# A projected tensor stored with 8 channels innermost between a projection and a depthwise convolution

## The chip, the cores and the metric

The kernel runs on one core of one Trainium2 chip. The metric is the device time of one execution in microseconds (us). Engines are named as the profile names them: PE is the matrix engine (PEld its weight loads), DVE the vector engine, ACT the scalar engine, POOL the GpSimd engine, SP the sync engine, which here only issues transfers. SBUF is the on-chip memory, PSUM the accumulator that PE writes.

## The reference

```python
# x: 16 images, 192 channels, 56 x 56
def _L0_conv_ref(x, ...):          # quantized window attention, windows of 7 x 7, 12 heads
    ...
    out = quant_linear(out, Wout, bout)                       # the projection
    return out.reshape(B, r1, r2, WS, WS, C).transpose(0, 5, 1, 3, 2, 4).reshape(B, C, H, W)

def _L1_conv_ref(x, ...):
    y = jax.lax.conv_general_dilated(x, dw_w, window_strides=(1, 1), padding=[(3, 3), (3, 3)],
                                     feature_group_count=C)   # 7 x 7, each channel by itself
    y = y + dw_b[None, :, None, None]
    ...                             # layer norm over channels, 192 -> 768, gelu, norm, 768 -> 192
    return residual + y
```

## The kernel before, in words

The kernel is a sequence of phases: `phase_input`, `phase_qkv_range`, `phase_qkv`, `phase_range`, `phase_attention`, `phase_project`, `phase_conv`, `phase_mlp`. Each writes its result to DRAM and the next reads it from there. Inside a phase every engine has its own instruction stream, written out by hand, and the streams meet at semaphores. The change touches `phase_project`, `phase_conv` and the DRAM tensor `yd` between them.

**phase_project** works on one image after the other, the buffers of two images in turn (index `k`). The attention result of an image comes as two units (`o_in`, 588 KB a transfer, four transfers an image), POOL rounds it to 16 bits (`o_int`, L1036), PE transposes it in bands of 7 image rows (L1082, 8 transposes of 128 columns a band, 8 bands an image, for the image that comes next), and DVE places each band into `oT` (L1202, two instructions a band). From `oT` two products are formed:

- `y` (L1098): the projection with a pair of image rows (two rows of 64 positions) on the 128 partitions and the 192 output channels in the free dimension. One step x of the loop makes two row pairs (q = 2x, 2x + 1), each out of two matmuls of 192 columns (96 + 3 and 96 input rows), in one PSUM bank; 29 row pairs make NY = 15 steps, of which the last has one pair. The moving operand is `woutT`, the stationary one `oT`. Two banks are used in turn, so PE waits at step x until DVE has done step x - 2 (semaphore `ye`).
- `r` (L1106): the same projection with channels on partitions, 448 positions at a time, 14 steps an image, two matmuls each. It is the residual and is evacuated by ACT (L1134).

The `y` product is kept as two 16-bit parts. ACT (L1125) writes the high part of both row pairs, 384 elements, in one instruction. DVE (L1215) then computes product times scale minus high part, one instruction of 192 elements a row pair, so two a step. The tile `y_out` is `[P, NCB, 2, CB, QP]`: 24 blocks of CB = 8 channels, the two parts, 8 channels, QP = 29 row pairs innermost. Neighbouring channels are therefore 29 elements, 58 bytes, apart, and ACT and DVE write (and DVE also reads) with that step. At the end of an image POOL issues the store of `y_out` to `yd` (L1047, 2784 KB) and of `r_out` to `rd` (L1049, 2352 KB).

PE's order in a step x is: the y matmuls, the r matmuls, then (x even) the transposes of one band of the next image. ACT's order is y part, r part. DVE's order is the low parts of step x, then (x even) the placing of a band.

**phase_conv** takes a block of 8 channels at a time, 24 blocks, double buffered: SP loads `c_in` from `yd` (1856 KB, all 16 images), two banded weight matrices (`toeplitz`, 1024 KB each, L1253) and the bias, after the block before the last has been evacuated. The convolution over the rows and columns of a row pair is a product with a 128 x 128 banded matrix; d = 0, 1, -1, 2 are the offsets in row pairs. Each channel takes 4 x 3 = 12 matmuls (L1282) into its own PSUM bank: three for each offset (high weight by high part, high by low, low by high), 448 columns for d = 0 and 1, 432 for d = -1 and 2. The moving operand is `c_in[:, images, part, ch, lo+d:hi+d]`, 16 runs of 28 or 27 neighbouring 16-bit elements, and every matmul has its own weight load. ACT evacuates a channel with L1296 into `c_out`, a 32-bit tile whose innermost dimension is the 8 channels, so with a step of 32 bytes. POOL stores the block (1792 KB, L1263).

**Other places that matter as comparisons.** In the attention and range phases the product L533 takes its stationary operand from `k_diag` with `[:, j::UP]`, UP = 16 elements of bf16, a step of 32 bytes over 128 columns. In `phase_qkv` DVE copies 8-bit values to bf16: L508 in order, L511 with the source read at a step of 49 bytes and written in runs of four. In `phase_mlp` L1485 and L1521 read 448 neighbouring elements as moving operand; L1688 is the same operation as L1215 (scale, subtract the high part, 16-bit result) on 448 neighbouring elements.

Of the kernel before, what the change touches and what calls it, by code (L numbers as in the profile page):

```python
# [39 lines left out]
CB = 8  # L40
# [39 lines left out]
def setup(nc, a, ctx):  # L80
# [22 lines left out]
    s.od = s.dram("od", [UNITS, 2, N, UP, 2, CK], F32)  # L103
    s.yd = s.dram("yd", [NCB, P, IMG, 2, CB, QP], F16)
    s.zd = s.dram("zd", [IMG, P, NCB, ROWP, CB], F32)
# [838 lines left out]
def phase_project(s):  # L944
# [3 lines left out]
    with ExitStack() as c:  # L948
# [4 lines left out]
        ot = [[sb(f"oT{t}_{k}", [CK + NPART * (t == 0), ROWS, PITCH], BF16) for t in range(2)] for k in range(2)]  # L953
        y = [sb(f"y_out{k}", [P, NCB, 2, CB, QP], F16) for k in range(2)]
        r = [sb(f"r_out{k}", [CK, 2, TOK], F32) for k in range(2)]
# [58 lines left out]
        def _(pool):  # L1014
# [24 lines left out]
            def image(i, first, has_next):  # L1039
                for k in range(2):  # L1040
                    m = 2 * i + k
                    if has_next(1):
                        for hf in range(2):
                            quantize(2 * m + 4 + hf, hf, False)
                    pool.wait_ge(ye, NY * (m + 1))
                    pool.wait_ge(re, 2 * NTC * (m + 1))
                    pool.dma_start(s.yd[:, :, bass.ds(m, 1)].rearrange("b p i x c q -> p (b i) (x c q)"),  # L1047
                                   y[k][:].rearrange("p b x c q -> p b (x c q)")).then_inc(sty[k], 16)
                    pool.dma_start(s.rd[bass.ds(m, 1)].rearrange("i (t p) n -> (i p) t n", t=2), r[k][:]).then_inc(strr[k], 16)  # L1049
# [10 lines left out]
        def _(pe):  # L1060
# [27 lines left out]
            def image(i, first, has_next):  # L1088
                for k in range(2):
                    m = 2 * i + k  # L1090
                    pe.wait_ge(otd, 16 * (m + 1))
                    for x in range(NY):
                        if not (first and k == 0 and x < 2):
                            pe.wait_ge(ye, NY * m + x - 1)
                        for qq in range(2 * x, min(2 * x + 2, QP)):
                            for t in range(2):
                                rows = ot[k][t][:, ROWS - 2 * qq - 2:ROWS - 2 * qq, :].rearrange("p r x -> p (r x)")
                                last = nc.tensor.matmul(py[:, (x + k * NY) % 2, qq % 2 * C:(qq % 2 + 1) * C], rows, s.woT[t][:],  # L1098
                                                        start=t == 0, stop=t == 1)
# [14 lines left out]
        def _(act):  # L1114
            act.wait_ge(ch, LCH)

            def image(i, first):
                for k in range(2):
                    m = 2 * i + k
                    for x in range(NY):  # L1120
                        act.wait_ge(ym, NY * m + x + 1)
                        if not first and x == 0:
                            act.wait_ge(sty[k], 16 * i)
                        nq = min(2, QP - 2 * x)
                        nc.scalar.activation(y[k][:, :, 0, :, 2 * x:2 * x + nq].rearrange("p b c q -> p q b c"),  # L1125
                                             py[:, (x + k * NY) % 2, 0:nq * C].rearrange("p (q b c) -> p q b c", b=NCB, c=CB),
                                             ACT.Copy, scale=ysc[:]).then_inc(yh, 1)
# [11 lines left out]
        def _(dve):  # L1139
# [67 lines left out]
            def image(i, first, has_next):  # L1207
                for k in range(2):
                    m = 2 * i + k
                    for x in range(NY):  # L1210
                        dve.wait_ge(yh, NY * m + x + 1)
                        nq = min(2, QP - 2 * x)
                        for qq in range(nq):
                            part = y[k][:, :, :, :, 2 * x + qq]
                            last = v.scalar_tensor_tensor(part[:, :, 1], py[:, (x + k * NY) % 2, qq * C:(qq + 1) * C].rearrange("p (b c) -> p b c", c=CB),  # L1215
                                                          ysc[:], part[:, :, 0], ALU.mult, ALU.subtract)
                        last.then_inc(ye, 1)
                        if has_next(k) and x % 2 == 0:
                            place(m + 1, 1 - k, x // 2, first and k == 0)
# [3 lines left out]
def phase_conv(s):  # L1223
# [5 lines left out]
    with ExitStack() as c:  # L1229
        sb = lambda n, sh, dt: c.enter_context(nc.sbuf_tensor(n, sh, dt))  # L1230
        yi = [sb(f"c_in{k}", [P, IMG, 2, CB, QP], F16) for k in range(2)]
        tp = [sb(f"toeplitz{k}", [P, 2, CB, D, P], F16) for k in range(2)]
# [9 lines left out]
        def _(sp):  # L1242
            def block(i, first):
                for k in range(2):
                    n = 2 * i + k
                    if not first:
                        sp.wait_ge(ev, CB * (n - 1))
                    sp.dma_start(yi[k][:], s.yd[bass.ds(n, 1)].rearrange("b p i x c q -> (b p) i x c q")).then_inc(ld[k], 16)
                    for x in range(2):
# [19 lines left out]
        def _(pe):  # L1269
            def block(i, first):  # L1270
                for k in range(2):
                    n = 2 * i + k
                    pe.wait_ge(ld[k], 64 * (i + 1))
                    for ch in range(CB):
                        if not (first and k == 0):
                            pe.wait_ge(ev, CB * (n - 1) + ch + 1)
                        out = ps[:, ch, 0:IMG * ROWP].rearrange("p (i r) -> p i r", i=IMG)

                        for x, d in enumerate((0, 1, -1, 2)):
                            lo, hi = max(0, -d), min(ROWP, QP - d)  # L1280
                            for part, (w, yy) in enumerate(((0, 0), (0, 1), (1, 0))):
                                last = nc.tensor.matmul(out[:, :, lo:hi], tp[k][:, w, ch, 2 - d, :], yi[k][:, :, yy, ch, lo + d:hi + d],  # L1282
                                                        start=x == 0 and part == 0, stop=x == 3 and part == 2)
                        last.then_inc(mm, 1)
# [515 lines left out]
```

## Time and profile before

| | |
|---|---|
| median of 3 runs | 6250.11 us (6248.59 to 6251.65) |
| the profiled execution, span from first to last instruction | 6255.8 us |
| PE busy | 4613.8 us (74%), 34250 instructions |
| DVE busy | 4853.0 us (78%), 8894 instructions |
| ACT busy | 3365.4 us (54%), 5458 instructions |
| POOL busy | 1553.1 us (25%), 1645 instructions |
| phase_project, by the first and last y product and low part | 3217 to 3822 us |
| wait for the last store and the first loads of the convolution | 3822 to 3859 us |
| phase_conv, its matmuls | 3859 to 4359 us |

For the profiled execution the trace gives the span alone; 6255.8 us is 5.7 us above the median of the runs. In the profile a row of the grouped view names line, engine, operation, out<-in, shapes and count, then the busy time in us and the mean of one in ns, then the idle time of the engine before them and what ended it. The granted PE clock is given as a share of full speed.

### The profile page before, as it was taken

To read this page: it belongs to the slowest core of one execution; us is meant where nothing else is said; L and a number is where in the kernel's file an instruction comes from. 1 tells how busy PE (TensorE), PEld (TensorE's weight loads), DVE (VectorE), ACT (ScalarE), POOL (GpSimd) and SP (SyncE) were. 2 spreads that over 40 slices of the span, in tenths; PEclk is the share of its full clock that TensorE was granted. 3 is DMA by queue.
4 is the path that set the end of the run, shared out by engine and by line. 5 is a ranking of instruction groups with operands and counts; after the bars stand their busy time and mean duration, and the time that the engine had idled before them with its cause. 6 is when DMAs were issued, how large, how long until landed. Compare 5 with 4: busy or idle time off the path is not lost. (4 is left out here: it accounts for less than half of the span.)

```text
span 6255.8 us, 106546 instructions
## 1 busy us (share of the span) xinstructions
PE 4613.8 (74%) x34250; PEld 2551.4 (41%) x34250; DVE 4853.0 (78%) x8894; ACT 3365.4 (54%) x5458; POOL 1553.1 (25%) x1645
## 2 busy tenths in 40 slices
PE   0879975555466666666647775998599998999989
PEld 0435543222255554554535453443233333333333
DVE  5989988999999888988968883000778778787784
ACT  1746650000177777777748885443455555555553
POOL 1013320000155555555532220000212112121120
PEclk9995555555599999999965556999799999999999
DMA  7846662333332222222235555887111212212111
GB/s 285 222 120 186 193 178 51 65 62 62 57 79 70 70 76 73 71 69 73 63 115 201 197 195 197 281 276 260 55 56 64 79 56 70 74 53 89 56 62 56
DMA packets 226353, 721.81 MB, mean 115 GB/s; under 512 B 34954, under 2 KB 132746, under 8 KB 205194
## 3 DMA queue, kind: packets, MB, share of 16 engines
q1 hardware_dynamic: 182346, 523.09, 29.3%
q0 software_dynamic: 43584, 193.63, 9.2%
q8 instruction: 197, 3.23, 0.2%
q14 instruction: 226, 1.85, 0.1%
HBM read 426.68 MB, written 289.92 MB: 115 GB/s over the span
## 5 line engine op out<-in xcount | busy, mean ns | idle before, releaser
L861 ACT ACTIVATE attn_int<-p_psum,scalars 128x588 int8<-128x588 f32 x512 | 384.2, 750 | 1174.9 <-PE p_psum L533 1174.2
L785 POOL TENSOR_TENSOR exp_lo<-exp,exp_hi 128x294 f16<-128x294 f32 x1024 | 826.9, 830 | 646.5 <-ACT exp_hi L855 644.8
L1570 ACT ACTIVATE gelu<-h_psum,b_rows,w_unscale 128x448 f32<-128x448 f32 x672 | 485.3, 722 | 669.7 <-PE h_psum L1485 548.6
L1521 PE MATMUL out_psum<-gelu_hi,w_parts 128*128 128x448 f16 x2016 | 622.3, 364 | 8.3 <-DVE w_parts L1707 4.4
L826 PE MATMUL o_psum<-a_v,exp_hi 128*128 128x68 f16 x3072 | 286.0, 202 | 444.9 <-DVE a_o L906 437.3
L533 PE MATMUL range_psum<-q_diag,k_diag 128*128 128x196 bf16 x1536 | 364.6, 373 | 331.0 <-DVE p_min L651 328.8
L1613 DVE BATCH_NORM_STATS2 ln_stats<-z_img 128x6 f32<-128x192 f32 x448 | 125.5, 337 | 555.7 <-DMA z_img<-zd 555.7
L1685 DVE TENSOR_SCALAR gelu_hi<-gelu,h_scale 128x448 f16<-128x448 f32 x672 | 323.5, 486 | 284.5 <-ACT gelu L1570 276.8
L1125 ACT ACTIVATE y_out<-y_psum,y_scale 128x384 f16<-128x384 f32 (+1 forms) x240 | 453.4, 1889 | 145.8 <-PE y_psum L1098 141.1
L1282 PE MATMUL conv_psum<-c_in,toeplitz 128*128 128x448 f16 (+1 forms) x2304 | 476.4, 369 | 62.2 <-DMA dwb<-in_L_conv_dw_b_dram 59.6
L1485 PE MATMUL h_psum<-ln_parts_T,w_hi 128*128 128x448 f16 x2016 | 502.0, 359 | 18.1 <-DVE w_in L1676 17.3
L880 DVE SCALAR_TENSOR_TENSOR logit_int<-attn_int,scalars,bias_products 128x588 f16<-128x588 int8 x512 | 442.9, 865 | 92.1 <-issue 58.8
L1215 DVE SCALAR_TENSOR_TENSOR y_out<-y_psum,y_scale,y_out 128x192 f16<-128x192 f32 x464 | 442.1, 1151 | 91.0 <-ACT y_out L1125 88.7
L1521 PE MATMUL out_psum<-gelu_lo,w_parts 128*128 128x448 f16 (+1 forms) x1344 | 499.6, 373 | 0.0
L1688 DVE SCALAR_TENSOR_TENSOR gelu_lo<-gelu,h_scale,gelu_hi 128x448 f16<-128x448 f32 x672 | 457.8, 695 | 0.0
L1485 PE MATMUL h_psum<-ln_parts_T,w_lo 128*128 128x448 f16 x1344 | 440.1, 361 | 0.0
L826 PEld LDWEIGHTS o_psum<-a_v,exp_hi 128*128 128x128 f16 x3072 | 220.8, 101 | 514.7 <-DVE a_o L906 477.6
L1296 ACT ACTIVATE c_out<-conv_psum,dwb,conv_unscale 128x448 f32<-128x448 f32 x192 | 223.4, 1163 | 315.2 <-PE conv_psum L1282 315.2
L854 ACT ACTIVATE exp<-l_psum,scalars 128x588 f32<-128x588 f32 x512 | 381.2, 744 | 21.7 <-PE l_psum L812 20.7
L855 ACT ACTIVATE exp_hi<-l_psum,scalars 128x588 f16<-128x588 f32 x512 | 391.9, 765 | 0.0
L533 PEld LDWEIGHTS range_psum<-q_diag,k_diag 128*128 128x128 bf16 x1536 | 180.9, 159 | 514.5 <-DVE p_min L651 511.1
L651 DVE TENSOR_TENSOR p_max<-range_psum,p_max 128x588 f32<-128x588 f32 x512 | 383.9, 750 | 0.0
(306 smaller groups left out, 10448.7 us busy)
## 6 DMA issues: line engine op xcount, KB each, us to landing
k_diag<-kd SPq DMA_DIRECT2D x128, 384.0 KB, 5.2
toeplitz<-gd SPq DMA_DIRECT2D x48, 1024.0 KB, 17.2
yd<-y_out POOLq DMA_DIRECT2D x16, 2784.0 KB, 20.9
c_in<-yd SPq DMA_DIRECT2D x24, 1856.0 KB, 9.1
zd<-c_out POOLq DMA_DIRECT2D x24, 1792.0 KB, 13.7
z_img<-zd SPq DMA_DIRECT2D x16, 2688.0 KB, 9.7
x_chunk<-in_x_dram SPq DMA_DIRECT2D x12, 3136.0 KB, 9.8
x_img<-in_x_dram SPq DMA_DIRECT2D x16, 2352.0 KB, 16.0
```

The source lines that it names most:

```text
L533: last = nc.tensor.matmul(out[:, g, 0:HG * N], kt[:, g].rearrange("p o n -> p (o n)")[:, j::UP], q[:, g, :, j * N:(j + 1) * N], start=True ...
L785: last = nc.gpsimd.tensor_tensor(el[r][:, :, a, 0:N], src[:, :, a], eh[r][:, :, a, 0:N], ALU.subtract)
L826: last = nc.tensor.matmul(po[:, b * PV0:(b + 1) * PV0], x[r][:, b].rearrange("p a n -> p (a n)"), rhs, start=x is eh, stop=x is el)
L855: nc.scalar.activation(eh[r][:].rearrange("p b a n -> p a b n")[:, :, :, 0:N], pl[:, bank, 0:HM].rearrange("p (a b n) -> p a b n", a=2, b= ...
L880: v.scalar_tensor_tensor(a2[r][:], a1[(l - LAG_A2) % 2][:], col(s, RAT), s.bpart[:], ALU.mult, ALU.add).then_inc(a2d, 1)
L1125: nc.scalar.activation(y[k][:, :, 0, :, 2 * x:2 * x + nq].rearrange("p b c q -> p q b c"), py[:, (x + k * NY) % 2, 0:nq * C].rearrange("p ...
L1215: last = v.scalar_tensor_tensor(part[:, :, 1], py[:, (x + k * NY) % 2, qq * C:(qq + 1) * C].rearrange("p (b c) -> p b c", c=CB), ysc[:], p ...
L1282: last = nc.tensor.matmul(out[:, :, lo:hi], tp[k][:, w, ch, 2 - d, :], yi[k][:, :, yy, ch, lo + d:hi + d], start=x == 0 and part == 0, sto ...
L1485: last = nc.tensor.matmul(ph[:, y % 3, 0:TCH], w, xx, start=x == 0, stop=x == 4)
L1521: last = nc.tensor.matmul(po[0:rows, t, 0:TCH], w, hx[:, f, cols], start=f == 0 and x == 0, stop=f == NF - 1 and x == len(steps) - 1)
L1570: nc.scalar.activation(h[y % 3][:], ph[:, y % 3, 0:TCH], ACT.Gelu, scale=k1[:], bias=b1[:, f:f + 1]).then_inc(hd, 1)
L1688: v.scalar_tensor_tensor(hl[:, f - 1, cols], h[(y - 1) % 3][:], kh[:], hh[:, f - 1, cols], ALU.mult, ALU.subtract).then_inc(hld, 1)
```

## The change

The dimension order of `yd`, `y_out` and `c_in` becomes row pairs, then channels: 8 channels are innermost (16 bytes). The y matmuls write their PSUM bank in the order block, row pair, channel, so that a block's row pairs lie next to each other. ACT's high part has runs of 16 neighbouring elements on both sides. DVE's low part becomes one instruction of 384 elements a step. The convolution's moving operand steps over row pairs, 8 elements or 16 bytes. Transfers, buffers, semaphores and their counts stay.

```diff
-    s.yd = s.dram("yd", [NCB, P, IMG, 2, CB, QP], F16)
+    s.yd = s.dram("yd", [NCB, P, IMG, 2, QP, CB], F16)
...
-        y = [sb(f"y_out{k}", [P, NCB, 2, CB, QP], F16) for k in range(2)]
+        y = [sb(f"y_out{k}", [P, NCB, 2, QP, CB], F16) for k in range(2)]
...
-                        for qq in range(2 * x, min(2 * x + 2, QP)):
+                        nq = min(2, QP - 2 * x)
+                        both = py[:, (x + k * NY) % 2, 0:nq * C].rearrange("p (b q c) -> p q b c", q=nq, c=CB)
+                        for qq in range(nq):
+                            top = ROWS - 2 * (2 * x + qq) - 2
                             for t in range(2):
-                                rows = ot[k][t][:, ROWS - 2 * qq - 2:ROWS - 2 * qq, :].rearrange("p r x -> p (r x)")
-                                last = nc.tensor.matmul(py[:, (x + k * NY) % 2, qq % 2 * C:(qq % 2 + 1) * C], rows, s.woT[t][:],
+                                rows = ot[k][t][:, top:top + 2, :].rearrange("p r x -> p (r x)")
+                                last = nc.tensor.matmul(both[:, qq], rows, s.woT[t][:].rearrange("p (b c) -> p b c", c=CB),
                                                         start=t == 0, stop=t == 1)
...
-                        nc.scalar.activation(y[k][:, :, 0, :, 2 * x:2 * x + nq].rearrange("p b c q -> p q b c"),
-                                             py[:, (x + k * NY) % 2, 0:nq * C].rearrange("p (q b c) -> p q b c", b=NCB, c=CB),
+                        nc.scalar.activation(y[k][:, :, 0, 2 * x:2 * x + nq, :].rearrange("p b q c -> p b (q c)"),
+                                             py[:, (x + k * NY) % 2, 0:nq * C].rearrange("p (b x) -> p b x", b=NCB),
                                              ACT.Copy, scale=ysc[:]).then_inc(yh, 1)
...
-                        for qq in range(nq):
-                            part = y[k][:, :, :, :, 2 * x + qq]
-                            last = v.scalar_tensor_tensor(part[:, :, 1], py[:, (x + k * NY) % 2, qq * C:(qq + 1) * C].rearrange("p (b c) -> p b c", c=CB),
-                                                          ysc[:], part[:, :, 0], ALU.mult, ALU.subtract)
-                        last.then_inc(ye, 1)
+                        hi, lo = (y[k][:, :, h, 2 * x:2 * x + nq, :].rearrange("p b q c -> p b (q c)") for h in range(2))
+                        v.scalar_tensor_tensor(lo, py[:, (x + k * NY) % 2, 0:nq * C].rearrange("p (b x) -> p b x", b=NCB),
+                                               ysc[:], hi, ALU.mult, ALU.subtract).then_inc(ye, 1)
...
-        yi = [sb(f"c_in{k}", [P, IMG, 2, CB, QP], F16) for k in range(2)]
+        yi = [sb(f"c_in{k}", [P, IMG, 2, QP, CB], F16) for k in range(2)]
...
-                                last = nc.tensor.matmul(out[:, :, lo:hi], tp[k][:, w, ch, 2 - d, :], yi[k][:, :, yy, ch, lo + d:hi + d],
+                                last = nc.tensor.matmul(out[:, :, lo:hi], tp[k][:, w, ch, 2 - d, :], yi[k][:, :, yy, lo + d:hi + d, ch],
                                                         start=x == 0 and part == 0, stop=x == 3 and part == 2)
```

The two transfers of `yd` (L1047 and L1248) follow the new order; each moves the same runs of neighbouring bytes as before.

## Rows read from the trace of the kernel before

**Rows 1.** Busy time by stretch: projection, gap, convolution, and a stretch of phase_qkv.
```profile
core 0: us, PE busy (x) PEld busy (x) DVE busy (x) ACT busy (x) POOL busy (x), PEclk, DMA share, GB/s
3217.00:3822.00 605.00, 437.16 (x2332) 291.93 (x2330) 513.04 (x704) 526.99 (x464) 122.42 (x90) 0.55 0.55 188
3822.00:3859.00 37.00, 0.51 (x2) 0.28 (x3) 0.00 (x0) 0.00 (x0) 2.10 (x2) 0.50 0.81 269
3859.00:4359.00 500.00, 475.86 (x2304) 224.80 (x2301) 0.00 (x0) 223.17 (x192) 26.55 (x23) 0.99 0.80 267
547.00:625.00 78.00, 77.88 (x324) 46.44 (x323) 76.56 (x117) 54.39 (x115) 30.64 (x36) 0.50 0.67 195
```

**Rows 2.** Waits in the projection: total us, times, longest.
```profile
PEld y_psum L1098 <- DVE y_out L1215: 256.7, 212, 3.4
...
PE y_psum L1098 <- DVE y_out L1215: 115.6, 159, 1.8
DVE y_out L1215 <- ACT y_out L1125: 88.7, 120, 3.0
```

**Rows 3.** Two steps of the projection in order of time (start us, us, instruction).
```profile
3500.49 1.94 DVE L1215 SCALAR_TENSOR_TENSOR y_out<-y_psum,y_scale,y_out 128x192 f16<-128x192 f32 x2 [0.38 <-ACT y_out L1125]
...
3502.49 0.82 PE L1098 MATMUL y_psum<-woutT,oT 99*128 99x192 bf16 x4 [0.75 <-DVE y_out L1215]
...
3503.10 0.95 PE L1106 MATMUL r_psum<-oT,woutT 99*96 99x448 bf16 x2
3503.34 1.93 ACT L1125 ACTIVATE y_out<-y_psum,y_scale 128x384 f16<-128x384 f32 x1
...
3503.85 1.06 PE L1082 MATMUL oT_psum<-ident_f,o_int 128*96 128x128 f16 x8
```

**Rows 4.** Groups by line and shape, whole trace: the projection's instructions and contiguous ones like them.
```profile
L1688 DVE SCALAR_TENSOR_TENSOR gelu_lo<-gelu,h_scale,gelu_hi 128x448 f16<-128x448 f32 x672 | 457.8, 695 | 0.0
...
L1215 DVE SCALAR_TENSOR_TENSOR y_out<-y_psum,y_scale,y_out 128x192 f16<-128x192 f32 x464 | 442.1, 1151 | 91.0 <-ACT y_out L1125 88.7
L1125 ACT ACTIVATE y_out<-y_psum,y_scale 128x384 f16<-128x384 f32 x224 | 435.9, 1946 | 145.8 <-PE y_psum L1098 141.1
...
L861 ACT ACTIVATE attn_int<-p_psum,scalars 128x588 int8<-128x588 f32 x512 | 384.2, 750 | 1174.9 <-PE p_psum L533 1174.2
...
L472 ACT ACTIVATE qk_i<-qk_psum,qk_quant_scale 128x392 int8<-128x392 f32 x384 | 196.6, 580 | 56.0 <-PE qk_psum L448 55.8
...
L1134 ACT ACTIVATE r_out<-r_psum,res_const,scale_y 96x448 f32<-96x448 f32 x224 | 195.1, 871 | 0.0
...
L1202 DVE TENSOR_SCALAR oT<-oT_psum 96x392 bf16<-96x392 f16 x256 | 131.7, 591 | 16.1 <-PE oT_psum L1082 16.1
```

**Rows 5.** Two stretches of 20.8 us inside the convolution.
```profile
3912.40:3933.20 20.80, 20.80 (x104) 10.05 (x103) 0.00 (x0) 9.84 (x9) 1.15 (x1) 1.00 0.77 243
3933.20:3954.00 20.80, 19.11 (x95) 8.99 (x93) 0.00 (x0) 8.78 (x8) 1.15 (x1) 1.00 0.91 308
```

**Rows 6.** PE alone in phase_mlp, contiguous moving operand (start us, us).
```profile
5001.44 0.54 PE L1521 MATMUL out_psum<-gelu_hi,w_parts 128*128 128x448 f16 x2
5001.82 0.35 PE L1521 MATMUL out_psum<-gelu_lo,w_parts 128*128 128x448 f16 x1
5002.01 0.54 PE L1521 MATMUL out_psum<-gelu_hi,w_parts 128*128 128x448 f16 x2
```

**Rows 7.** Groups by line and shape, whole trace: instructions with a step, and their contiguous neighbours.
```profile
L1570 ACT ACTIVATE gelu<-h_psum,b_rows,w_unscale 128x448 f32<-128x448 f32 x672 | 485.3, 722 | 669.7 <-PE h_psum L1485 548.6 <-issue 121.1
...
L1296 ACT ACTIVATE c_out<-conv_psum,dwb,conv_unscale 128x448 f32<-128x448 f32 x192 | 223.4, 1163 | 315.2 <-PE conv_psum L1282 315.2
...
L511 DVE CAST k_out<-qk_i 128x392 bf16<-128x392 int8 x128 | 129.5, 1012 | 4.0
...
L508 DVE CAST q_out<-qk_i 128x392 bf16<-128x392 int8 x128 | 45.6, 356 | 0.0
```

**Rows 8.** Weight loads in the attention phase: contiguous (L826) and with a 32-byte step (L533).
```profile
L826 PEld LDWEIGHTS o_psum<-a_v,exp_lo 128*128 128x128 f16 x2940 | 220.3, 100 | 0.0
...
L533 PEld LDWEIGHTS p_psum<-q_diag,k_diag 128*128 128x128 bf16 x1470 | 152.0, 149 | 73.6 <-issue 73.6
```

More of the change, by code:

```diff
@@ L1046, in image @@
                     pool.wait_ge(re, 2 * NTC * (m + 1))
-                    pool.dma_start(s.yd[:, :, bass.ds(m, 1)].rearrange("b p i x c q -> p (b i) (x c q)"),
-                                   y[k][:].rearrange("p b x c q -> p b (x c q)")).then_inc(sty[k], 16)
+                    pool.dma_start(s.yd[:, :, bass.ds(m, 1)].rearrange("b p i x q c -> p (b i) (x q c)"),
+                                   y[k][:].rearrange("p b x q c -> p b (x q c)")).then_inc(sty[k], 16)
                     pool.dma_start(s.rd[bass.ds(m, 1)].rearrange("i (t p) n -> (i p) t n", t=2), r[k][:]).then_inc(strr[k], 16)
@@ L1247, in block @@
                         sp.wait_ge(ev, CB * (n - 1))
-                    sp.dma_start(yi[k][:], s.yd[bass.ds(n, 1)].rearrange("b p i x c q -> (b p) i x c q")).then_inc(ld[k], 16)
+                    sp.dma_start(yi[k][:], s.yd[bass.ds(n, 1)].rearrange("b p i x q c -> (b p) i x q c")).then_inc(ld[k], 16)
                     for x in range(2):
```

## The prediction

> **What bounds the kernel now.** I cut the span into phases first, because the change touches two of them and leaves the other six as they are. The busy time by stretch [rows 1] shows the projection, 605 us: ACT busy 527 us, DVE 513 us, PE 437 us at a granted clock of 0.55 (so mostly at 1.2 GHz), the DMA engines 55% of the time. No engine is full, so the bound must be a loop between them. The waits [rows 2] name it: PE's y product waits 115.6 us for DVE's low part (its weight load 256.7 us), DVE 88.7 us for ACT's high part. Two PSUM banks are used in turn, so step x + 2 of PE needs DVE's step x. The order in time [rows 3] gives one turn: DVE's two low parts from 3500.49 for 1.94 us, PE's four matmuls from 3502.49 for 0.82 us, ACT's high part from 3503.34 for 1.93 us, then DVE again at about 3505.3: 4.8 us for two steps, 2.4 a step. 15 steps and a boundary make 605/16 = 37.8 us an image.
>
> The convolution is different. Its 500 us have PE busy 476 us at clock 0.99, with the DMA engines at 80% [rows 1]. In its full stretches 104 matmuls start in 20.8 us, in the others 95 [rows 5]: 200 ns a matmul, or 219 where loads are late. 96 matmuls at 200 ns are 19.2 us of the 500/24 = 20.8 us of a block. PE sets this phase almost alone, and the transfers follow closely.
>
> So the change makes cheaper what bounds the projection and touches, in the convolution, the one operand whose streaming bounds that phase.
>
> **The projection, removed work.** The low part: 464 instructions of 1151 ns go [rows 4], 240 of 384 elements come. The same operation on 448 neighbouring elements costs 695 ns (L1688) [rows 4]. Fewer elements, but one operand from PSUM: I take 650 ns. The high part: 1946 ns now for 384 elements with a 58-byte step. Contiguous evacuations with one scale cost 580 ns for 392 elements and 750 for 588 [rows 4]; I take 600 ns. Runs of 16 instead of one long run may add a little; the ends are 550 ns and 900.
>
> **What is next in line there.** Four sums for one image, in its engines' own durations:
> - PE: 58 y matmuls of 192 columns, 28 r matmuls of 448, 64 transposes of 128, together 31,872 columns. At the half clock, which 0.55 says it nearly always has, these are 26.6 us. (Check in [rows 3]: 8 transposes in 1.06 us, 107 ns apart plus one latency.)
> - ACT: 15 x 0.60 + 14 x 0.87 (L1134 [rows 4]) = 21.2 us.
> - DVE: 15 x 0.65 + 16 x 0.59 (L1202 [rows 4]) = 19.2 us.
> - DMA: 0.55 x 605/16 = 20.8 us of pure transfer.
>
> PE becomes the longest. The old loop shrinks to 0.65 + 0.82 + 0.60 = 2.1 us for two steps, but in the worst order it also waits behind ACT's r part (0.87) and DVE's placing (1.2): 4.1 us for two steps, 31 us an image, against 3.5 for PE's columns. PE alone with 1.8 us for the turn of images (last band transposed, placed, first product) gives 28.4 us. I take the middle, 29.7 us, 475 us in all: **130 us saved**. Ends: 31 us an image and more trouble with the transfers, 60 us saved; or the clock goes to its upper level and ACT's 21.2 us bind, 340 us, 265 saved. Against that second end speaks a stretch of phase_qkv where PE is busy 77.88 of 78 us and the clock still reads 0.50 [rows 1]: a fuller PE does not by itself bring the upper level.
>
> POOL's order (round two units, wait for the image, issue the two stores) is not moved; its roundings wait for PE's transposes and come earlier with them. SP's loads likewise. The stores keep their runs of bytes, so L1047's packets cost what they did. The y matmuls now write PSUM in runs of 8 columns with a gap of 8: the nearest row is the convolution's own, which writes 16 runs, and I cost it at nothing; if each such write took double, 58 x 192 columns would add 9.3 us an image and take the whole gain of this phase. PE has no cover for it once it is the bound.
>
> **The convolution, the changed read.** 2304 matmuls of 440 columns on average. Now one takes 200 ns: 183 ns of columns at 2.4 GHz plus 17. In phase_mlp, with one contiguous run of 448, three matmuls start in 5002.01 - 5001.44 = 0.57 us, 190 ns each against 187 of columns [rows 6]. So 16 short runs already cost some 14 ns more than one long one, about 0.9 ns at each jump. After the change each of the 440 elements is its own jump of 16 bytes. No row shows a moving operand with a step; the bounds:
> - Below: nothing. The trace has no step as short as 16 bytes, and the jumps above may have another cause.
> - By PE's jumps: 0.9 ns an element, 396 ns more a matmul, 38 us a block, 24 x 38 = 912 us, less the 1.6 us a block that PE now waits: some 870.
> - By ACT's writes with a 32-byte step: 1163 ns against 722 for 448 elements [rows 7], 0.98 ns more an element. A contiguous element costs ACT (750 - 580)/196 = 0.87 ns [rows 4], so a step costs it a little over double per element.
> - By DVE's read with a 49-byte step: 1012 against 356 ns for 392 elements [rows 7], 1.67 ns more; on PE 735 ns a matmul, some 1690 us. This is the upper end.
> - By PE's own other read: 128 weight columns at a 32-byte step take 149 ns against 100 [rows 8], 0.38 ns more a column, which nearly doubles PE's 0.42 ns.
>
> ACT's ratio (its element time slightly over doubled) and PE's weight loads (0.38 ns more a column) agree, and the last row is the nearest since it is PE reading 16-bit data from SBUF. I take a doubled column: 440 x 0.83 = 367 ns plus 8, 375 ns a matmul, 36.0 us a block. Transfers (0.80 x 20.8 = 16.7 us a block) and ACT (8 x 1.16 = 9.3 us) lie well inside. 24 x 36.0 = 864 us instead of 500: **364 us lost**.
>
> The Trainium skill has a rule on this (page "SBUF — State Buffer", section "Door 1: The DMA port swizzle", the note on cachelines): SBUF has lines of 16 bytes, full bandwidth wants at least two accesses to a line, and every move to a new line is penalised. By it the change falls exactly on one access a line, and the sum is of the sign that I give. ACT's row with a 32-byte step agrees.
>
> The gap of 37 us between the phases (store and first load) keeps its length; phase_mlp reads `zd`, which is unchanged.
>
> **The sum.** -130 + 364 = +234 us. On the profiled span: 6255.8 + 234 = 6490; the runs' median is 5.7 us lower, so 6484 us. With the bounds of this case (60 to 265 saved; 0.8 to 0.9 ns a column, 340 to 410 lost), its own range is 6325 to 6600.
>
> **Rivals.**
> - *The 16-byte step is free.* The convolution stays 500 us and only the projection moves: 6250 - 130 = 6120, or 5985 to 6190. This is faster, by one mechanism in one place: PE's fetch of the moving operand at L1282. It decides from a price of about 0.6 ns a column: the gain of 130 us over 24 x 96 x 440 = 1.01 million columns is 0.13 ns each, on top of today's 200/440 = 0.45. For it: 16 bytes is shorter than every step in rows 7 and 8, and weight loads could be slower for reasons of their own. Against it: three different engines pay for a step in this trace. The same note of the Trainium skill also says that 8 bf16 elements can be strided for free; taken at its word that is this rival, 6120 us, and no run here shows it yet.
> - *The step costs three times or more a column.* By PE's jump price 6250 - 130 + 870 = 6990, by DVE's read up to 7810. For it: the jump price is from the very same matmuls. Against it: the weight loads, where 128 such columns fit in 149 ns altogether, latency included.
> - *The projection gains nothing*, because PSUM writes in runs of 8 columns double the y matmuls, or the loop of waits stays: then +364 stands alone, 6614. For: nothing in the rows; against: the sizes of L1215 and L1125, which can only fall.
>
> **How the numbers follow.** Doubled column 0.46; free step (with mild prices below 0.6 ns) 0.35; three times or more 0.16; no gain in the projection beside a slow convolution 0.03. The likeliest case gives the time, 6484 us. To hold 8 in 10 the range must take in the free step's middle and leave out the third case: 6030 to 6600. Faster by over 0.2% (12.5 us, about what a measurement of this kernel can tell from no change): 0.35. Within: 0.01. Slower: 0.64.
>
> **What would show it.** L1282: start to start near 375 ns and a convolution phase near 864 us, its mean duration some 180 ns above 373; if it stays at 200 ns, the free step is right; near 600, the third case. The granted clock of that phase is of interest, since a read-bound PE would not need the upper level. L1215 as 240 instructions near 650 ns, L1125 near 600. In the projection the waits of L1098 on L1215 nearly gone, PE over 90% busy at 0.5 to 0.6, and 475 us. If L1098's matmuls start further apart than 160 ns, the PSUM pattern costs something. The prediction is wrong if a column of the convolution costs under 0.6 ns.

## The result: 18% slower, and the profile after

The changed kernel takes 7395.85 us, median of 4 runs (7381.1 to 7400.09), against 6250.88 us for the kernel before in its 4 runs. The ratio is 1.1826 with a 95% interval of 1.1809 to 1.1843. The forecast was 6484 us with a range of 6030 to 6600. The change is slower, as forecast, but by 1145 us instead of 234, and the time lies outside the range.

The busy time by stretch, after the change (columns: stretch, length, then busy time and count for PE, weight loads, DVE, ACT, POOL; granted PE clock, DMA share, GB/s). It answers to [rows 1].

```profile
3217.00:3661.00 444.00, 271.94 (x2367) 200.51 (x2365) 221.95 (x488) 254.78 (x463) 122.41 (x90) 0.79 0.72 256
3661.00:3699.00 38.00, 0.03 (x1) 0.00 (x0) 1.04 (x2) 0.98 (x3) 2.10 (x2) 0.55 0.82 273
3699.00:5492.00 1793.00, 1792.80 (x2304) 289.88 (x2304) 0.00 (x0) 222.12 (x192) 26.56 (x23) 0.50 0.22 75
```

The projection fell from 605 to 444 us, the gap stayed (37 and 38), and the convolution rose from 500 to 1793 us. -161 + 1293 = +1132 us; the spans differ by 7390.9 - 6255.8 = 1135. Nothing else moved by more than a few us. In the convolution PE is busy all the time, its clock is at the lower level, and the DMA engines are at 22% where they were at 80%.

The same from the page of the changed kernel: lines 1 and 2, with a digit for each fortieth of the span.

```profile
span 7390.9 us, 106322 instructions
...
PE 5765.3 (78%) x34250; PEld 2524.2 (34%) x34250; DVE 4562.2 (62%) x8670; ACT 3096.7 (42%) x5458; POOL 1552.6 (21%) x1645
...
DVE  6989889999899988854400000000017887887885
...
PEclk9975555559999989977755555555558999999999
DMA  7746533323222222247721212121211212212211
```

DVE has 224 instructions fewer, as the diff says. The row of zeros in DVE's line is the convolution; it covers nine slices where it covered three. Over the same slices the clock stands at 5.

The groups of the changed instructions, over the whole trace (line, engine, operation, shapes, count | busy us, mean ns | idle before, releaser). They answer to [rows 4].

```profile
L1283 PE MATMUL conv_psum<-c_in,toeplitz 128*128 128x448 f16 x1152 | 947.6, 971 | 38.0 <-DMA dwb<-in_L_conv_dw_b_dram 38.0
L1283 PE MATMUL conv_psum<-c_in,toeplitz 128*128 128x432 f16 x1152 | 913.7, 942 | 0.0
...
L1137 ACT ACTIVATE r_out<-r_psum,res_const,scale_y 96x448 f32<-96x448 f32 x224 | 166.2, 742 | 64.2 <-DMA rd<-r_out 60.3 <-PE r_psum L1109 3.6
...
L1217 DVE SCALAR_TENSOR_TENSOR y_out<-y_psum,y_scale,y_out 128x384 f16<-128x384 f32 x224 | 136.0, 607 | 211.6 <-ACT y_out L1128 211.3
...
L1128 ACT ACTIVATE y_out<-y_psum,y_scale 128x384 f16<-128x384 f32 x224 | 133.4, 595 | 189.6 <-PE y_psum L1101 97.3 <-DMA yd<-y_out 92.2
```

The low part costs 607 ns for 384 elements instead of twice 1151, the high part 595 instead of 1946. The convolution's matmul, in the kernel before:

```profile
L1282 PE MATMUL conv_psum<-c_in,toeplitz 128*128 128x448 f16 x1152 | 272.6, 373 | 62.2 <-DMA dwb<-in_L_conv_dw_b_dram 59.6 <-ACT c_out L1296 2.6
```

It went from 373 ns (366 with 432 columns) to 971 and 942. Those means include a latency that overlaps with the next matmul; the price is the distance from start to start. Weight loads of the changed kernel, one for each matmul (start us, us, [idle before]):

```profile
4000.19 0.13 PEld L1283 LDWEIGHTS conv_psum<-c_in,toeplitz 128*128 128x128 f16 x1 [0.67 <-issue]
4000.98 0.13 PEld L1283 LDWEIGHTS conv_psum<-c_in,toeplitz 128*128 128x128 f16 x1 [0.67 <-issue]
4001.77 0.12 PEld L1283 LDWEIGHTS conv_psum<-c_in,toeplitz 128*128 128x128 f16 x1 [0.66 <-issue]
```

0.79 us a matmul of 448 columns; over the phase 1793/2304 = 778 ns for 440 columns, 1.77 ns a column, where a matmul took 200 ns in full stretches before [rows 5].

The waits of the projection after the change (engine, line, waited for: total us, times, longest). They answer to [rows 2].

```profile
DVE y_out L1217 <- ACT y_out L1128: 214.9, 160, 15.5
...
ACT y_out L1128 <- DMA yd<-y_out: 92.2, 7, 16.0
PE y_psum L1101 <- DVE y_out L1217: 78.4, 17, 13.4
ACT r_out L1137 <- DMA rd<-r_out: 60.3, 8, 11.4
```

Two lines are new: ACT waits seven times, up to 16 us, until the store of `y_out` of two images ago has ended, and eight times for that of `r_out`. These waits existed before in the code and cost nothing. Together they are 152 us of 444. The stores take longer too: from issue to landing the median is 29.5 us for yd and 36.5 for rd, where it was 20.9 and 29.0 us.

### The profile page after: what moved, and what is told of

Its sections match the earlier page's. It is cut to its first block and busy times, and to the rows that moved or that the text cites. A ratio compares the mean times of both kernels' runs of the same rounds, so it can differ in the third digit from the quotient of the medians.

```text
span 7390.9 us, 106322 instructions
## 1 busy us (share of the span) xinstructions
PE 5765.3 (78%) x34250; PEld 2524.2 (34%) x34250; DVE 4562.2 (62%) x8670; ACT 3096.7 (42%) x5458; POOL 1552.6 (21%) x1645
## 5 line engine op out<-in xcount | busy, mean ns | idle before, releaser
L1283 PE MATMUL conv_psum<-c_in,toeplitz 128*128 128x448 f16 (+1 forms) x2304 | 1792.8, 957 | 38.0 <-DMA dwb<-in_L_conv_dw_b_dram 38.0
L1283 PEld LDWEIGHTS conv_psum<-c_in,toeplitz 128*128 128x128 f16 x2304 | 289.9, 126 | 1539.6 <-issue 1501.3
L826 PE MATMUL o_psum<-a_v,exp_hi 128*128 128x68 f16 x3072 | 286.5, 202 | 446.7 <-DVE a_o L906 439.0
L533 PE MATMUL range_psum<-q_diag,k_diag 128*128 128x196 bf16 x1536 | 364.8, 373 | 330.8 <-DVE p_min L651 328.6
L1264 POOL DMA_DIRECT2D zd<-c_out x24 | 27.7, 1155 | 1802.3 <-ACT c_out L1297 1802.3
L826 PEld LDWEIGHTS o_psum<-a_v,exp_hi 128*128 128x128 f16 x3072 | 221.3, 101 | 516.7 <-DVE a_o L906 479.9
L651 DVE TENSOR_TENSOR p_min<-range_psum,p_min 128x588 f32<-128x588 f32 x512 | 387.1, 756 | 0.0
## 6 DMA issues: line engine op xcount, KB each, us to landing
yd<-y_out POOLq DMA_DIRECT2D x16, 2784.0 KB, 29.5
```

Of the source, the lines that this page charges most:

```text
L651: v.tensor_tensor(e[:], ps[:, j % 4, 0:G, 0:HG * N], e[:], op).then_inc(done, 1)
L826: last = nc.tensor.matmul(po[:, b * PV0:(b + 1) * PV0], x[r][:, b].rearrange("p a n -> p (a n)"), rhs, start=x is eh, stop=x is el)
```

## The experiments

Two questions were open. The first: is the whole loss PE's read, and what does a step cost? The second: what bounds the projection now? Except where said, an experiment is compared with runs of the kernel before on the same chip; those medians were 6258 us (e1 to e4), 6254 (e5 to e8) and 6253 (e9, e10), each group on a chip of its own.

### Taking the change apart: e1 and e2

e1 is the changed kernel in which only the convolution's moving operand is read in runs again. The elements are others of the same block, so its convolution isn't the reference's.

```diff
-  yi[k][:, :, yy, lo + d:hi + d, ch]
+  yi[k][:, :, yy].rearrange("p i q c -> p i (q c)")[:, :, ch * QP + lo + d:ch * QP + hi + d]
```

> The changed kernel, with the convolution's moving operand read in runs of 27 or 28 neighbouring elements again (other elements of the same block, so the convolution's result is another one); layout, transfers and projection stay as changed. If the whole loss is PE's read with the 16-byte step: convolution back at 500 us, projection at 444 us as in the changed kernel, total 6250.9 - 161 = 6090 us. If part of the loss comes with the layout of c_in or its transfers, the convolution stays above 520 us.

e2 is the kernel before, with the step put into its read alone (other elements here too).

```diff
-  yi[k][:, :, yy, ch, lo + d:hi + d]
+  yi[k][:, :, yy].rearrange("p i c q -> p i (c q)")[:, :, ch + CB * (lo + d):ch + CB * (hi + d - 1) + 1:CB]
```

> The kernel before, with the moving operand read with a step of 8 elements (16 bytes) over the same block (other elements, another result); projection as before. If the read alone makes the loss: convolution 1793 us, total 6250.9 + 1293 = 7544 us, and with e1 the two parts of the change add up to the change. If layout matters: convolution clearly off 1793.

e1 took 6105.37 us (ratio 0.9753, interval 0.9737 to 0.9769), e2 7552.12 us (1.2066, 1.2042 to 1.209; two runs). The instructions that write `conv_psum` in e1 and in e2 (durations min/median/max in ns, first and last start in us):

```profile
L1283 PE MATMUL conv_psum<-c_in,toeplitz x2304: 350/353/581, 3708.8 to 4206.8; 128*128 128x448 f16 x192
```

```profile
L1282 PE MATMUL conv_psum<-c_in,toeplitz x2304: 942/948/976, 3863.0 to 5654.9; 128*128 128x448 f16 x192
```

The convolution lasts 498 us in e1 and 1792 us in e2, so the layout of the tile and its transfers play no part in the loss. The ratios add up: -2.5% and +20.7% against +18.3% for the change.

### What a step costs: e3 to e7

e3 and e4 keep the idea of the change with 4 and with 2 channels innermost, so the convolution's step is 8 or 4 bytes. They compute the reference. The two parts stand inside the group of channels, so that DVE's operands keep two free dimensions:

```diff
+CG = 4                                     # e4: 2
-  yd [NCB, P, IMG, 2, QP, CB]     y_out [P, NCB, 2, QP, CB]     c_in [P, IMG, 2, QP, CB]
+  yd [NCB, P, IMG, CB // CG, 2, QP, CG]     y_out [P, C // CG, 2, QP, CG]     c_in [P, IMG, CB // CG, 2, QP, CG]
-  yi[k][:, :, yy, lo + d:hi + d, ch]
+  yi[k][:, :, ch // CG, yy, lo + d:hi + d, ch % CG]
```

> Four channels innermost instead of eight: the projection writes runs of 8 elements, the convolution reads with a step of 8 bytes, two elements from each 16-byte line. Theory of lines (each new 16-byte line costs PE about 1.7 ns, shared by the elements in it): 0.83 to 0.88 ns a column, convolution 880 to 940 us, total about 6500. Theory of two hits (a line that is hit twice costs nothing): convolution 500 us, total about 6090. Theory of the step (any step costs about the same as 16 bytes): convolution near 1793 us, total near 7390.

> Two channels innermost: the projection writes runs of 4 elements (8 bytes), the convolution reads with a step of 4 bytes, four elements a line. Theories of lines and of two hits: convolution 500 to 530 us. Theory of the step: near 1793. The projection between the changed kernel's 444 us and before's 605, since runs of 4 elements may cost ACT and DVE more: total 6090 to 6250.

e3 took 6518.15 us (1.0406, 1.0381 to 1.0431), e4 6123.46 us (0.9778, 0.9762 to 0.9794). The stretches of projection and convolution in e3, then in e4:

```profile
3219.00:3670.00 451.00, 269.96 (x2336) 199.00 (x2336) 218.66 (x480) 255.10 (x463) 122.52 (x90) 0.78 0.72 252
3708.00:4629.00 921.00, 921.00 (x2304) 267.26 (x2302) 0.00 (x0) 224.07 (x191) 26.56 (x23) 1.00 0.44 145
```

```profile
3227.00:3680.00 453.00, 270.58 (x2335) 200.17 (x2336) 219.83 (x480) 254.61 (x462) 122.53 (x90) 0.79 0.71 250
3719.00:4233.00 514.00, 504.90 (x2304) 225.30 (x2304) 0.00 (x0) 222.30 (x192) 26.56 (x23) 1.00 0.78 261
```

With the 8-byte step PE is busy throughout, a matmul takes 921/2304 = 400 ns, about half of 778. With 4 bytes the phase is back within 14 us of before. Two elements a line are not enough; the theory of two hits would have given 500 us. Note the clock in e3: 1.00. The runs that ACT and DVE write shrink from 32 bytes to 16 and 8, and the projection keeps nearly all of its gain (451 and 453 us against 444).

e5 is the kernel before with another step for each channel of a block, in one run (other elements, another result):

```diff
+  flat = yi[k][:].rearrange("p i x c q -> p i (x c q)")
-  yi[k][:, :, yy, ch, lo + d:hi + d]
+  flat[:, :, (lo + d) * S:(hi + d - 1) * S + 1:S]        # S = ch + 1
```

> The kernel before, with the moving operand of channel 0 of each block read with a step of 1 element (2 bytes), of channel 1 with 2 elements, and so on to channel 7 with 8 elements (16 bytes), each over other elements of the same block, so the convolution's result is another one. Theory of lines, with 1.77 ns for each 16-byte line that a run touches: start to start 200, 213, 304, 403, 488, 594, 679 and 778 ns a matmul for steps of 1 to 8 elements, 43.9 us a block, convolution 1052 us, total 6251 + 552 = 6800 us. Theory of a threshold at 16 bytes: steps 1 to 7 at 200 ns, step 8 at 778, 26.1 us a block, total about 6380. Theory of two hits: steps 1 to 4 at 200 ns.

It took 6858.65 us (one run). ACT evacuates a channel as soon as its 12 matmuls are done, so the distance between two evacuations is their price. ACT alone, one block (start us, us):

```profile
4234.81 1.17 ACT L1348 ACTIVATE c_out<-conv_psum,dwb,conv_unscale 128x448 f32<-128x448 f32 x1 [2.18 <-PE conv_psum L1286]
4237.28 1.17 ACT L1348 ACTIVATE c_out<-conv_psum,dwb,conv_unscale 128x448 f32<-128x448 f32 x1 [1.31 <-PE conv_psum L1293]
4240.98 1.18 ACT L1348 ACTIVATE c_out<-conv_psum,dwb,conv_unscale 128x448 f32<-128x448 f32 x1 [2.53 <-PE conv_psum L1300]
4245.78 1.17 ACT L1348 ACTIVATE c_out<-conv_psum,dwb,conv_unscale 128x448 f32<-128x448 f32 x1 [3.62 <-PE conv_psum L1307]
4251.71 1.16 ACT L1348 ACTIVATE c_out<-conv_psum,dwb,conv_unscale 128x448 f32<-128x448 f32 x1 [4.77 <-PE conv_psum L1314]
4258.89 1.18 ACT L1348 ACTIVATE c_out<-conv_psum,dwb,conv_unscale 128x448 f32<-128x448 f32 x1 [6.02 <-PE conv_psum L1321]
4267.01 1.16 ACT L1348 ACTIVATE c_out<-conv_psum,dwb,conv_unscale 128x448 f32<-128x448 f32 x1 [6.94 <-PE conv_psum L1328]
4276.35 1.16 ACT L1348 ACTIVATE c_out<-conv_psum,dwb,conv_unscale 128x448 f32<-128x448 f32 x1 [8.18 <-PE conv_psum L1335]
4280.83 1.17 ACT L1348 ACTIVATE c_out<-conv_psum,dwb,conv_unscale 128x448 f32<-128x448 f32 x1 [3.32 <-PE conv_psum L1286]
```

The row at 4234.81 is channel 0, step 1. The differences that follow, divided by 12:

| step, bytes | 16-byte lines a matmul (mean) | expected, 1.77 ns a line | measured, ns a matmul |
|---|---|---|---|
| 4 | 120 | 213 | 206 |
| 6 | 172 | 304 | 308 |
| 8 | 228 | 403 | 400 |
| 10 | 276 | 488 | 494 |
| 12 | 336 | 594 | 598 |
| 14 | 384 | 679 | 677 |
| 16 | 440 | 778 | 778 |

The lines are counted from the pattern: 16 runs of 28 or 27 elements, each run starting at a line or one or two steps behind it. One constant fits seven steps within 3.5%. In the 24 blocks of the run the distances for steps of 6 to 16 bytes repeat within 0.01 us; only that for 4 bytes varies, from 2.47 to 2.74 us (206 to 228 ns), and the block shown has the shortest. Up to 16 bytes there is no threshold and no free second hit: the times are as if PE got a new line every 1.77 ns or so and a column waited if its line isn't there. No trace shows the fetch itself. With a step of 2 bytes there are 64 lines, 113 ns, and the columns themselves (183 ns) are longer.

The total is 59 us over the expectation, and the last row above gives a part of it: channel 0 of the next block takes 4.48 us, 373 ns a matmul instead of 200. The clock during channel 7 of the block before, then during channels 3 (8 bytes), 7 (16 bytes) and the next channel 0:

```profile
4222.00:4231.00 9.00, 9.00 (x13) 1.42 (x12) 0.00 (x0) 1.16 (x1) 0.00 (x0) 0.50 0.00 0
...
4241.00:4245.80 4.80, 4.80 (x13) 1.39 (x12) 0.00 (x0) 1.18 (x2) 0.00 (x0) 1.00 1.02 401
...
4267.00:4276.30 9.30, 9.30 (x13) 1.50 (x12) 0.00 (x0) 1.16 (x1) 0.00 (x0) 0.50 0.00 0
4276.40:4280.80 4.40, 4.40 (x13) 1.74 (x12) 0.00 (x0) 1.11 (x1) 1.15 (x1) 0.50 0.52 132
```

The 8-byte step runs at the upper level and costs 400 ns here as in e3. While the longest steps run the clock falls to its lower level, and the dense matmuls behind them start at 1.2 GHz: 448/1.2 = 373 ns. This block is one of the dearest: over the 23 blocks whose channel 0 has another block ahead of it, that channel takes 3.24 to 4.57 us, 3.82 in the mean, where 12 matmuls of 200 ns are 2.40. So the clock gives some 1.4 us a block, 34 of the 59 us; the rest stays unexplained here.

e6 asks whether the lower clock is the cause of the slow read or goes beside it. Stepped matmuls are mixed with dense ones (other elements, another result):

```diff
-  yi[k][:, :, yy, ch, lo + d:hi + d]
+  flat[:, :, (lo + d) * S:(hi + d - 1) * S + 1:S]        # S = 8 for 1, 1, 2, 2, 3, 3, 4, 4 of the 12 matmuls of channels 0 to 7, else 1
```

> The kernel before, with 1, 1, 2, 2, 3, 3, 4 and 4 of the 12 matmuls of channels 0 to 7 read with the 16-byte step and the others with runs of neighbouring elements (other elements, another result): 20 stepped and 76 dense matmuls a block, so that PE's clock can be at its upper level while the stepped ones run. Theory of a fixed time for a line, whatever PE's clock: a stepped matmul takes 778 ns at the upper level too, 76 x 0.2 + 20 x 0.778 = 30.8 us a block, convolution about 740 us, total about 6490. Theory of two array cycles a column, doubled by the lower clock: 367 ns at the upper level, 22.5 us a block, convolution about 540 us, total about 6290.

It took 6484.65 us (one run). The convolution as a stretch, and inside it PE's matmuls and weight loads in order of time (L1342 reads with the step, L1340 in runs):

```profile
3861.00:4590.00 729.00, 725.05 (x2304) 233.17 (x2304) 0.00 (x0) 222.58 (x192) 27.11 (x24) 1.00 0.55 184
```

```profile
4216.93 0.95 PE L1342 MATMUL conv_psum<-c_in,toeplitz 128*128 128x448 f16 x1
...
4217.70 0.59 PE L1340 MATMUL conv_psum<-c_in,toeplitz 128*128 128x448 f16 x2
...
4218.12 0.95 PE L1342 MATMUL conv_psum<-c_in,toeplitz 128*128 128x448 f16 x1
```

At a granted clock of 1.00 the stepped matmul still takes 4217.70 - 4216.93 = 0.77 us for 448 columns, 1.72 ns a line, while its dense neighbours take 0.21. In the changed kernel, at 0.50, it took 0.79. The price is a time, not a number of array cycles. The rival, two cycles a column doubled by the lower clock, is out: it expected 367 ns. The lower clock in the changed kernel goes beside the slow read and doesn't cause it.

e7 tries longer steps, the same edit with S = 8, 9, 10, 12, 14, 15, 16, 16 (other elements, another result).

> The kernel before, with steps of 8, 9, 10, 12, 14, 15, 16 and 16 elements (16 to 32 bytes) for channels 0 to 7 (other elements, another result). Theory of lines: each element has a line of its own at all of these, 778 ns a matmul for each channel, convolution 1793 us, total 7544 us. If the distance counts beyond one line (a skipped line costs as well): rising towards 1500 ns a matmul at 16 elements, convolution towards 2700 us.

It took 7573.89 us (one run), 22 us above e2. ACT's evacuations in one block: of the channel before it and of channel 0 (8 elements), then of channels 4, 5 and 6, read with steps of 14, 15 and 16 elements:

```profile
4159.77 1.17 ACT L1348 ACTIVATE c_out<-conv_psum,dwb,conv_unscale 128x448 f32<-128x448 f32 x1 [8.30 <-PE conv_psum L1335]
4169.19 1.17 ACT L1348 ACTIVATE c_out<-conv_psum,dwb,conv_unscale 128x448 f32<-128x448 f32 x1 [8.26 <-PE conv_psum L1286]
...
4206.95 1.15 ACT L1348 ACTIVATE c_out<-conv_psum,dwb,conv_unscale 128x448 f32<-128x448 f32 x1 [8.36 <-PE conv_psum L1314]
4216.50 1.15 ACT L1348 ACTIVATE c_out<-conv_psum,dwb,conv_unscale 128x448 f32<-128x448 f32 x1 [8.40 <-PE conv_psum L1321]
4225.95 1.15 ACT L1348 ACTIVATE c_out<-conv_psum,dwb,conv_unscale 128x448 f32<-128x448 f32 x1 [8.30 <-PE conv_psum L1328]
```

The distances are 9.55 us for 15 elements and 9.45 us for 16, against 9.42 us for 8 elements in the same block. Over all blocks the means for steps of 8 to 16 elements lie between 773 and 796 ns a matmul. Skipped lines cost nothing, and from 16 bytes on the price is flat within 3%.

### What bounds the projection now: e8 to e10

These three start from e4, which took 6123.46 us.

e8 adds bytes to the stores and nothing else:

```diff
+  pool.dma_start(s.rd2[bass.ds(m, 1), 0:CK].rearrange("i p n -> (i p) n"), r[k][:, 0]).then_inc(strr[k], 16)
-  strr[k], 16 * i          # ACT's wait, and the last wait likewise
+  strr[k], 32 * i
```

> The kernel with two channels innermost, and half of the residual stored a second time to a scratch tensor at the end of each image (1176 KB more, semaphore counts raised), nothing else changed. Theory that the stores now bound the projection (ACT waits for y_out and r_out to be stored): 1176 KB at the 330 to 370 GB/s of the busiest slices is 3.2 to 3.7 us an image, projection 453 + 16 x 3.5 = 509 us, total 6123 + 56 = 6180. Theory that ACT, PE and DVE themselves bound it: projection stays at 453 us, total 6123 us.

It took 6189.49 us (0.9892, 0.9861 to 0.9923; two runs, on another chip than e4), 66 us more than e4. First and last y product, and ACT's waits on the stores:

```profile
L1104 PE MATMUL y_psum<-woutT,oT x928: 246/247/368, 3216.6 to 3722.3; 99*128 99x192 bf16 x93, 96*128 96x192 bf16 x93
```

```profile
ACT r_out L1140 <- DMA rd<-r_out: 166.3, 14, 19.0
...
ACT y_out L1131 <- DMA yd<-y_out: 49.1, 7, 15.7
```

The projection grew from 453 to 506 us; 1176 KB at the end of an image cost 3.3 us each time. The gap before the convolution, which waits for the last store, grew too, from 39 to 55 us. In e4 ACT waited 95 + 71 us for the stores, here 49 + 166. The stores bound the phase.

e9 gives the same bytes to the queue earlier:

```diff
-  for hf in range(2):
-      quantize(2 * m + 4 + hf, hf, False)
+      quantize(2 * m + 4, 0, False)
+  pool.wait_ge(re, 2 * NTC * m + 2 * 4)
+  pool.dma_start(... rd of image m, columns 0 : 4 * TCH ..., r[k][:, :, 0:4 * TCH]).then_inc(strr[k], 16)
+      quantize(2 * m + 5, 1, False)
...
-  pool.dma_start(... rd of image m ..., r[k][:]).then_inc(strr[k], 16)
+  pool.dma_start(... columns 4 * TCH : ..., r[k][:, :, 4 * TCH:]).then_inc(strr[k], 16)
```

> The kernel with two channels innermost, and the residual of an image stored in two parts: the first 4 of 7 chunks as soon as they are evacuated, between POOL's two roundings, the rest at the end of the image. Same bytes. Theory that the stores come too late in a burst at the end of each image and ACT waits for them: the burst falls from 5136 to 3790 KB, the waits of ACT on y_out and r_out (95 + 71 us) go mostly away, projection 453 us down to 380 to 410, total 6060 to 6090. Theory that the mean transfer rate bounds it: no change, 6123 us. Rival: POOL's first store waits for the residual and delays the second rounding, so PE's transposes come late: above 6123.

It took 6101.01 us (5 runs, 6098.08 to 6106.44; ratio 0.9757, 0.9744 to 0.977), the lowest time of this study. That is 22 us less than e4 by the medians and some 13 us by the ratios (0.9757 against 0.9778, whose intervals overlap, on different chips), so the total alone doesn't show a gain over e4. From the first to the last y product it takes 432 us, where e4 takes 453, in one trace each. Its waits:

```profile
ACT y_out L1133 <- DMA yd<-y_out: 105.7, 7, 18.3
...
POOL tick L1037 <- DMA o_in<-od: 79.2, 15, 7.3
...
ACT r_out L1142 <- DMA rd<-r_out: 39.5, 9, 5.7
```

The gain is smaller than the 380 to 410 us that was expected for the projection. The wait on r_out fell from 71 to 40 us, that on y_out didn't (95 to 106), and POOL now waits 79 us for `o_in` where it waited 47, so part of the burst may have moved onto the loads; that wasn't tested. The store of y_out, which can't be split in time without short runs, is what is left.

e10 undoes the other half of the change's title, one DVE instruction for two row pairs, and keeps the short step of the elements:

```diff
-  v.scalar_tensor_tensor(lo, ... 0:nq * C ..., ysc[:], hi, ALU.mult, ALU.subtract).then_inc(ye, 1)
+  for qq in range(nq):                     # one row pair each, 192 elements
+      last = v.scalar_tensor_tensor(lo, ..., ysc[:], hi, ALU.mult, ALU.subtract)
+  last.then_inc(ye, 1)
```

> The kernel with two channels innermost, but the low part as two DVE instructions of 192 elements a step, as in the kernel before. The 192-element form took 417 ns at the end of each image, so two cost 834 instead of 608 ns. If the merging itself was what freed the projection: DVE per image 15 x 0.83 + 16 x 0.48 = 20.2 us, still below the 28 us an image, so at most the undisturbed stretches of 1.07 us a step get longer (to about 1.3): projection 453 to 480 us, total 6123 to 6150. If only the short step of the elements mattered: no change, 6123.

6115.3 us (0.977, 0.9755 to 0.9785), the same as e4 within the intervals. Its low part:

```profile
L1219 DVE SCALAR_TENSOR_TENSOR y_out<-y_psum,y_scale,y_out 128x192 f16<-128x192 f32 x464 | 170.5, 408 | 199.9 <-ACT y_out L1129 191.4
```

The same 464 instructions that cost 1151 ns each before cost 408 in the new layout. So the gain of the projection comes from where neighbouring elements lie. The merging saves DVE another 28 us of busy time (170.5 us against 136.2 in e4 for the 224 merged instructions and, at 417 ns each, 7 us for the 16 single ones), and the total shows nothing of it.

## Why the prediction was wrong

**Right.** The loop of the projection and its end, the sizes of the new instructions (607 and 595 ns against 650 and 600), the phases left alone, the gap, that PSUM writes in short runs cost nothing (at the upper clock four y matmuls start in 0.34 us, from 3410.68 to 3411.02 us of the changed kernel's trace, 85 ns each for 192 columns, which are 80 ns at 2.4 GHz), and that PE's moving read decides in the convolution against the change. The sign followed from that.

**The term that failed: "I take a doubled column", 375 ns a matmul, +364 us.** It measured 778 ns and +1293 us. That a step costs PE time was right; the size was wrong, and so was the row chosen as nearest. I took the weight loads with a 32-byte step, 0.38 ns more a column [rows 8], because they are PE's reads too, and ACT's ratio of a little over two [rows 7]. The moving operand paid 1.77 ns a column in all, 1.3 ns more than before. ACT's row of the convolution, read as a time, was close: 0.87 + 0.98 = 1.85 ns an element with a step. I turned it into a ratio and multiplied it with PE's 0.42 ns, as if the price shrank with the faster engine. e6 shows that the read doesn't follow PE's clock. That 1.85 lies so near 1.77 may be chance, though: the high part, the same engine with a 58-byte step, cost (1946 - 595)/384 = 3.5 ns more an element than in runs, and DVE's low part (1151 - 408)/192 = 3.9. No single price per stepped element holds for all engines in this case, and a common cause isn't shown. The rows on those two instructions stood among the rows before [rows 4], and the sum for the convolution didn't use them.

**The jump price** of 0.9 ns [rows 5, 6] was from the very matmuls in question and gave +870 us. It had 0.16 with the rest of its case and was left out of the range. It was nearer than the value taken. The range for the convolution, 340 to 410 us lost, was a little narrow even for its own terms: 0.8 to 0.9 ns a column and 8 ns a matmul give 329 to 431.

**The rivals.** The third one is what came, three times or more a column: 1.77 ns against 0.45, and 7396 us lies between its 6990 and 7810. That the projection gains nothing is out (444 us). The free step is out (e2). In the Trainium skill, page "SBUF — State Buffer", section "Door 1: The DMA port swizzle", the note says that at least two hits on a line are needed for full bandwidth and that 8 bf16 elements can be strided for free. The lines themselves agree with the trace: one constant per 16-byte line fits e5. The two numbers don't hold for PE: two hits a line cost 400 ns where dense runs cost 200, and a step of 8 elements costs 778 ns, as much as any longer one.

**The projection, -130.** It measured -161, inside its ends of 60 and 265. That it came so near was in part luck: two statements behind it failed and worked against each other. I kept PE at its lower clock, on the stretch of phase_qkv [rows 1]; the mean was 0.79, and in full stretches it is at 1.00. And I had the transfers at 20.8 us an image, well inside the time of the others; they are the bound now, since both stores leave in one burst when an image ends and ACT needs the buffer two images on. The point that I priced as a mean share was one of timing. Stretches of the changed kernel, one in full flow and one while ACT waits for the store of y_out:

```profile
3410.00:3419.00 9.00, 8.56 (x87) 6.23 (x84) 7.42 (x17) 9.00 (x18) 3.00 (x2) 1.00 0.39 126
3392.00:3401.00 9.00, 0.82 (x4) 0.43 (x4) 1.33 (x3) 0.58 (x1) 0.00 (x0) 0.50 0.83 311
```

ACT is full in the first, 9.00 of 9 us, and the DMA engines are at 39%; in the second PE, DVE and ACT stand still at 83%.

**Not tried.** Copying `c_in` on DVE or POOL, which are idle or nearly so in the convolution, to give PE runs of neighbouring elements with 8 channels innermost in DRAM. e1 (6105 us) shows what a dense read would be worth beside this projection, if the copy cost nothing: 18 us less than e4.

## What to carry to other kernels

Count the 16-byte lines that PE's moving operand touches, not only its columns: in these runs a matmul took about the longer of its columns at the granted clock and 1.77 ns for each line, so with 16-bit data a step of 2 elements is nearly free, 4 doubles the price and 8 nearly quadruples it (200, 206 to 228, 400 and 778 ns). A layout that two phases share can often stop half-way: 2 channels innermost kept nearly the whole gain of the writer (453 against 444 us, from 605) and cost the reader 14 us. When a price is borrowed from another engine, borrow the nanoseconds and not the ratio, and where the rows of the very instruction give a price, put it inside the range.

## What the runs showed of the hardware beyond that

- PE can be busy for 1793 us without a gap while its granted clock stays at 0.50, when each matmul of 440 columns takes 778 ns; with 400 ns a matmul (e3) it was at 1.00 all the time. A full PE line in the page is no sign of the upper clock.
- After such a stretch dense matmuls start at the lower clock: up to 381 ns a matmul instead of 200 for channel 0 in e5, 318 in the mean, some 34 us over the run.
- Writes with a 58-byte step of 16-bit elements were dear: 1946 ns for 384 elements on ACT, and 595 in runs of 8, 16 and 32 bytes alike (e4, e3 and the change). Other instructions of the phase fell too, without being changed: r_out from 871 to 742 ns, an instruction that places a band from 591 to 476. That they had waited for the stepped writes of the others is likely and wasn't tested.
